# Inverse transforms in groups of four tiles, with one PSUM bank for each product

## The reference

```python
x = x + hyena(layernorm(x))          # out_w, out_b at its end
x = x + adapters(layernorm(x))       # 8 of 32 matrices W[ids], mixed by weights, and their bias

# hyena: v = short convolution of (x @ in_proj)[..., 0]; a filter h from a small network of the position
output = x_branches[i] * irfft(rfft(v, 2L) * rfft(h, 2L))[:, :L]    # only the last branch counts
return output @ out_w + out_b
```

## Time and profile before

| | |
|---|---|
| median of 3 runs | 2408.13 us (2402.51 to 2411.54) |
| the profiled execution | 2405.93 us, its span 2404.1 us |
| TensorE busy | 2314.3 us, 96% of the span |
| VectorE / ScalarE / GpSimd busy | 64% / 35% / 39% |
| the last stage | from about 1427 us to the end |

### The profile page before, as it was taken

The page is one execution under the profiler, slowest core; times in us unless marked ns, Lnnn a source line. Parts: engine busy times, 40 slices in busy tenths (PEclk is TensorE's granted clock), DMA queues, the critical chain, the costliest instruction groups (busy, mean ns, idle before and its releaser), DMA issues.

```text
span 2404.1 us, 39766 instructions
## 1 busy us (share of the span) xinstructions
PE 2314.3 (96%) x12804; PEld 1601.3 (67%) x12804; DVE 1547.2 (64%) x2187; ACT 843.4 (35%) x1151; POOL 946.2 (39%) x1190
## 2 busy tenths in 40 slices
PE   6679999999999999999999979999999999999998
PEld 2257777777777777644444426777777777777776
DVE  5834444443444344377777757888888888888886
ACT  3334444444444444344444432222222222222222
POOL 2322222222222222200000026777777777777774
PEclk9879999999999999999999989999999999999999
DMA  6634555445554555589999997855666665665663
GB/s 186 218 101 141 181 174 179 147 156 187 175 168 140 170 168 202 230 316 361 358 358 355 359 360 217 252 176 176 179 177 176 176 177 175 177 180 176 178 179 101
DMA packets 180517, 496.60 MB, mean 207 GB/s; under 512 B 19419, under 2 KB 19740, under 8 KB 159332
## 3 DMA queue, kind: packets, MB, share of 16 engines
q1 hardware_dynamic: 150756, 395.10, 51.3%
q10 hardware_dynamic: 29696, 100.68, 11.6%
HBM read 276.27 MB, written 219.43 MB: 206 GB/s over the span
## 4 chain that ended last, share of the span: by engine, by line
PE 52%; DVE 2%; issue 2%; DMA 1%; ACT 0%; DVEq 0%; POOL 0%; SPq 0%; POOLq 0%
PE m_psW L992 7%; PE m_psA L975 6%; PE b_psF L183 5%; PE b_psC L1290 5%; PE b_psF L184 5%; PE b_psO L184 5%; PE b_psO L183 5%; PE b_psO L185 5%; PE b_psF L185 5%; PE b_psP L1304 2%; PE b_psT L1321 2%; DVE m_m L1063 2%; DMA m_xin<-spec 1%; DMA spec<-wide_out 0%; DMA b_fin<-spec 0%
## 5 line engine op out<-in xcount | busy, mean ns | idle before, releaser
L1063 DVE TENSOR_TENSOR m_m<-m_psA,m_spec 128x1024 f32<-128x1024 f32 x256 | 295.4, 1215 | 110.5 <-PE m_psA L975 107.1
L720 POOL TENSOR_TENSOR vl<-v,vh 128x512 fp32r<-128x512 f32 x128 | 165.3, 1291 | 390.0 <-ACT vh L674 390.0
L1254 ACT ACTIVATE b_zh<-b_psT 128x512 fp32r<-128x512 f32 x128 | 76.4, 597 | 641.0 <-PE b_psT L1321 641.0
L992 PE MATMUL m_psW<-m_m,mats 64*64 64x512 f32 x2048 | 249.2, 589 | 0.0
L975 PE MATMUL m_psA<-m_xin,mats 64*64 64x512 f32 x1536 | 204.8, 598 | 11.2 <-DVE m_m L1063 5.5
L183 PE MATMUL psV<-wvh,nth 128*128 128x512 f32 x512 | 213.6, 417 | 0.6 <-DVE ntl L802 0.6
L821 DVE TENSOR_TENSOR gto<-psG,bgr 128x512 f32<-128x512 f32 x128 | 87.6, 685 | 195.4 <-PE psG L185 195.2
L183 PE MATMUL b_psO<-woh,b_oh 128*128 128x512 f32 x512 | 212.2, 414 | 0.0
L183 PE MATMUL b_psF<-wfh,b_zh 128*128 128x512 f32 x512 | 207.6, 406 | 2.8 <-DVE b_zl L1383 2.8
L184 PE MATMUL b_psO<-wol,b_oh 128*128 128x512 f32 x512 | 201.6, 394 | 0.0
L185 PE MATMUL b_psO<-woh,b_ol 128*128 128x512 f32 x512 | 201.4, 393 | 0.0
(11 more groups left out here) (126 smaller groups left out, 4696.4 us busy)
## 6 DMA issues: line engine op xcount, KB each, us to landing
spec<-wide_out SPq DMA_DIRECT2D x64, 1024.0 KB, 9.2
spec<-wide_out ACTq DMA_DIRECT2D x64, 1024.0 KB, 8.5
b_fin<-spec SPq DMA_DIRECT2D x128, 512.0 KB, 4.7
m_xin<-spec SPq DMA_DIRECT2D x30, 2048.0 KB, 11.9
xg<-in_L_attn_x_dram SPq DMA_DIRECT2D x64, 512.0 KB, 6.2
gate_d<-gto SPq DMA_DIRECT2D x32, 1024.0 KB, 3.9
b_gin<-gate_d SPq DMA_DIRECT2D x128, 256.0 KB, 3.6
b_xin<-in_L_attn_x_dram SPq DMA_DIRECT2D x256, 128.0 KB, 3.2
```

The source lines that it names most:

```text
L720: pool.tensor_tensor(vl[:, t % 2], v[:, t % 2], vh[:, t % 2].bitcast(F32), ALU.subtract).then_inc(v_lo, 1)
L992: mm = pe.matmul(psW[pair % 2][half[slot], q, :], ws[slot][half[q]], m[half[q], pair % RM, part, slot, :], start=part == 0, stop=part == 1)
L1063: dve.tensor_tensor(m[:, (k - 2) % RM, part], psA[k % RA][:], spec[:, par, part], ALU.mult).then_inc(m_done, 1)
```

## The change

The transforms of four tiles stand together in every fourth round (`conv_four`). Each of the four has a PSUM bank of its own; for these, psO and psF have one bank each instead of two. `b_fin` gets four buffers. All steps behind the transform have lags larger by three; `load_gate` and `load_x` have lag 2 instead of 0. `turn_w` uses the one bank of psO and the one of psF as scratch, so that the first project waits until that is over.

```diff
-            psC = [ps("b_psC0"), ps("b_psC1")]
+            psC = [ps(f"b_psC{i}") for i in range(4)]
-            psO = [ps("b_psO0"), ps("b_psO1")]
+            psO = ps("b_psO")
-            psF = [ps("b_psF0"), ps("b_psF1")]
+            psF = ps("b_psF")
+            psW = [psO, psF]
...
+            def fin_of(t):
+                return fin[:, t % 4] if t % 4 < 2 else fin_b[:, t % 4 - 2]
...
                 def load_conv(b, t):
...
-                    if old(b, t, 2):
-                        sp.wait_ge(c_ps, no(b, t) - 1)
+                    if old(b, t, 4):
+                        sp.wait_ge(c_ps, no(b, t) - 3)
...
-                pipelined(sp, B, T, [(load_conv, 0), (load_edges, 0), (load_gate, 0), (load_x, 0), (load_v0, 0)])
+                pipelined(sp, B, T, [(load_conv, 0), (load_edges, 0), (load_gate, 2), (load_x, 2), (load_v0, 0)])
...
-                pipelined(pool, B, T, [(correct, 0), (scalars, 3), (bias_y, 3)])
+                pipelined(pool, B, T, [(correct, 3), (scalars, 6), (bias_y, 6)])
...
-                pipelined(act, B, T, [(z_high, 4), (o_high, 1), (norm, 3), (w_high, 0), (store, 6)])
+                pipelined(act, B, T, [(z_high, 7), (o_high, 4), (norm, 6), (w_high, 0), (store, 9)])
...
                 def conv(b, t):
-                    pe.wait_ge(f_in[t % 2], 16 * (b * (T // 2) + t // 2 + 1))
-                    if old(b, t, 2):
-                        pe.wait_ge(a_done, no(b, t) - 1)
+                    pe.wait_ge(f_in[t % 4], 16 * (b * (T // 4) + t // 4 + 1))
+                    if old(b, t, 4):
+                        pe.wait_ge(a_done, no(b, t) - 3)
...
-                def conv_pair(b, t):
+                def conv_four(b, t):
...
-                    if t % 2:
-                        conv(b, t - 1)
-                        conv(b, t)
+                    if t % 4 == 3:
+                        for k in range(t - 3, t + 1):
+                            conv(b, k)
...
                 def project(b, t):
                     pe.wait_ge(o_lo, no(b, t) + 1)
-                    if old(b, t, 2):
-                        pe.wait_ge(y_done, no(b, t) - 1)
+                    if isinstance(b, int) and b * T + t == 0:
+                        pe.wait_ge(wf_lo, CT)
+                    if old(b, t, 1):
+                        pe.wait_ge(y_done, no(b, t))
...
                 def adapt(b, t):
...
-                    if old(b, t, 2):
-                        pe.wait_ge(res_done, no(b, t) - 1)
+                    if old(b, t, 1):
+                        pe.wait_ge(res_done, no(b, t))
...
-                pipelined(pe, B, T, [(conv_pair, 0), (turn_w, 0), (adapt, 5), (turn_z, 4), (turn_o, 1), (project, 2)])
+                pipelined(pe, B, T, [(conv_four, 0), (turn_w, 0), (adapt, 8), (turn_z, 7), (turn_o, 4), (project, 5)])
...
-                pipelined(dve, B, T, [(gate, 1), (residual, 3), (z_low, 4), (o_low, 1), (finish, 5), (bias_x, 0), (w_low, 0)])
+                pipelined(dve, B, T, [(gate, 4), (residual, 6), (z_low, 7), (o_low, 4), (finish, 8), (bias_x, 3), (w_low, 0)])
```

More of the change, by code:

```diff
@@ L1087, in back @@
             v0 = sb("b_v0", [P, B, C])
+            fin_b = sb("b_fin_b", [P, 2, 2, C])
             edge_b = sb("b_edge_b", [P, T - EARLY, 2, C])
@@ L1170, in load_conv @@
                         return
-                    if old(b, t, 2):
-                        sp.wait_ge(c_ps, no(b, t) - 1)
-                    sp.dma_start(fin[:, t % 2], spec3.rearrange("(r h t) b c -> b t r h c", h=2, t=T)[b, t]).then_inc(f_in[t % 2], 16)
+                    if old(b, t, 4):
+                        sp.wait_ge(c_ps, no(b, t) - 3)
+                    sp.dma_start(fin_of(t), spec3.rearrange("(r h t) b c -> b t r h c", h=2, t=T)[b, t]).then_inc(f_in[t % 4], 16)
                 def load_gate(b, t):
@@ L1263, in w_high @@
                         act.wait_ge(wf_ps, d + 1)
-                        act.activation(wfh[:, d], psF[d % 2][:], ACT.Copy).then_inc(wf_hi, 1)
-                pipelined(act, B, T, [(z_high, 4), (o_high, 1), (norm, 3), (w_high, 0), (store, 6)])
+                        act.activation(wfh[:, d], psW[d % 2][:], ACT.Copy).then_inc(wf_hi, 1)
+                pipelined(act, B, T, [(z_high, 7), (o_high, 4), (norm, 6), (w_high, 0), (store, 9)])
                 for i in range(D):
@@ L1281, in turn_w @@
                         for ot in range(CT):
-                            mm = pe.transpose(psF[d % 2][:, ot * P:(ot + 1) * P], res[:, ot, d * P:(d + 1) * P], ident[:])
+                            mm = pe.transpose(psW[d % 2][:, ot * P:(ot + 1) * P], res[:, ot, d * P:(d + 1) * P], ident[:])
                         mm.then_inc(wf_ps, 1)
                 def conv(b, t):
-                    pe.wait_ge(f_in[t % 2], 16 * (b * (T // 2) + t // 2 + 1))
-                    if old(b, t, 2):
-                        pe.wait_ge(a_done, no(b, t) - 1)
+                    pe.wait_ge(f_in[t % 4], 16 * (b * (T // 4) + t // 4 + 1))
+                    if old(b, t, 4):
+                        pe.wait_ge(a_done, no(b, t) - 3)
                     for h in range(2):
-                        mm = pe.matmul(psC[t % 2][h * N1:(h + 1) * N1, :], s4[:, h * T + t, :], fin[:, t % 2, h, :], start=True, stop=True)
+                        mm = pe.matmul(psC[t % 4][h * N1:(h + 1) * N1, :], s4[:, h * T + t, :], fin_of(t)[:, h, :], start=True, stop=True)
                     mm.then_inc(c_ps, 1)
-                def conv_pair(b, t):
-                    if t % 2:
-                        conv(b, t - 1)
-                        conv(b, t)
+                def conv_four(b, t):
+                    if t % 4 == 3:
+                        for k in range(t - 3, t + 1):
+                            conv(b, k)
                 def turn_o(b, t):
@@ L1308, in project @@
                     pe.wait_ge(o_lo, no(b, t) + 1)
-                    if old(b, t, 2):
-                        pe.wait_ge(y_done, no(b, t) - 1)
+                    if isinstance(b, int) and b * T + t == 0:
+                        pe.wait_ge(wf_lo, CT)
+                    if old(b, t, 1):
+                        pe.wait_ge(y_done, no(b, t))
                     for ct in range(CT):
-                        mm = mm3(pe, psO[t % 2][:], oh[:, t % 2, ct * P:(ct + 1) * P], ol[:, t % 2, ct * P:(ct + 1) * P],
+                        mm = mm3(pe, psO[:], oh[:, t % 2, ct * P:(ct + 1) * P], ol[:, t % 2, ct * P:(ct + 1) * P],
                                  woh[:, ct], wol[:, ct], ct == 0, ct == CT - 1)
@@ L1327, in adapt @@
                         pe.wait_ge(wf_lo, CT)
-                    if old(b, t, 2):
-                        pe.wait_ge(res_done, no(b, t) - 1)
+                    if old(b, t, 1):
+                        pe.wait_ge(res_done, no(b, t))
                     for ct in range(CT):
-                        mm = mm3(pe, psF[t % 2][:], zh[:, t % 2, ct * P:(ct + 1) * P], zl[:, t % 2, ct * P:(ct + 1) * P],
+                        mm = mm3(pe, psF[:], zh[:, t % 2, ct * P:(ct + 1) * P], zl[:, t % 2, ct * P:(ct + 1) * P],
                                  wfh[:, ct], wfl[:, ct], ct == 0, ct == CT - 1)
                     mm.then_inc(ff_ps, 1)
-                pipelined(pe, B, T, [(conv_pair, 0), (turn_w, 0), (adapt, 5), (turn_z, 4), (turn_o, 1), (project, 2)])
+                pipelined(pe, B, T, [(conv_four, 0), (turn_w, 0), (adapt, 8), (turn_z, 7), (turn_o, 4), (project, 5)])
             @block.vector
@@ L1343, in w_low @@
                         dve.wait_ge(wf_hi, d + 1)
-                        dve.tensor_tensor(wfl[:, d], psF[d % 2][:], wfh[:, d].bitcast(F32), ALU.subtract).then_inc(wf_lo, 1)
+                        dve.tensor_tensor(wfl[:, d], psW[d % 2][:], wfh[:, d].bitcast(F32), ALU.subtract).then_inc(wf_lo, 1)
                 def bias_x(b, t):
@@ L1353, in gate @@
                     dve.wait_ge(c_ps, no(b, t) + 1)
-                    dve.tensor_tensor(corr[:, t % 2], psC[t % 2][:], corr[:, t % 2], ALU.add).then_inc(a_done, 1)
+                    dve.tensor_tensor(corr[:, t % 2], psC[t % 4][:], corr[:, t % 2], ALU.add).then_inc(a_done, 1)
                     dve.wait_ge(a_done, no(b, t) + 1)
@@ L1370, in residual @@
                         dve.wait_ge(z_done, no(b, t) - 1)
-                    dve.tensor_tensor(y[:, t % 2], psO[t % 2][:], xin[:, t % D], ALU.add).then_inc(y_done, 1)
+                    dve.tensor_tensor(y[:, t % 2], psO[:], xin[:, t % D], ALU.add).then_inc(y_done, 1)
                     dve.wait_ge(y_done, no(b, t) + 1)
@@ L1389, in finish @@
                         dve.wait_ge(out_stored[t % D], 32 * (b * (T // D) + t // D))
-                    dve.tensor_tensor(res[:, t % D], psF[t % 2][:], yb[:, t % D], ALU.add).then_inc(res_done, 1)
-                pipelined(dve, B, T, [(gate, 1), (residual, 3), (z_low, 4), (o_low, 1), (finish, 5), (bias_x, 0), (w_low, 0)])
+                    dve.tensor_tensor(res[:, t % D], psF[:], yb[:, t % D], ALU.add).then_inc(res_done, 1)
```

(3 more changed lines are left out.)

## The result

The changed kernel takes 2413.73 us (median of 20 runs, 2405.13 to 2419.25), the kernel before 2407.60 us (median of 20 on the same chip). The ratio is 1.0024, 95% interval 1.0016 to 1.0031: 6 us slower, a quarter of a per cent. The forecast was 2418 us, with a range of 2396 to 2437. The interval excludes "no change", so the kernel is slower, but by less than the half per cent that the prediction used as its border: of its three cases "within 0.5%" came true, which had a chance of 0.40, where "slower" had 0.49.

What follows compares the result with a forecast made beforehand. TensorE's own order was taken as the bound (busy 868.00 of 868.00 us). 2405.9 - 13.1 + 25.4 - 4 + 1.5 = 2415.7, on the median's scale 2418 us; range 2396 to 2437.

Steps and rivals of the forecast that it cites:

- The group's price: TensorE, last stage: each group of transforms costs 0.41 us beyond its work; 32 fewer groups save 13.1 us.
- The rival of the slower adapt: TensorE's adapt after transforms: its extra 0.17 us follows the tiles, so only 7.7 us saved, 2423 us; chance 0.10.
- The late fourth load: SyncE's queue: each group's fourth-tile load, behind x loads waiting for y, comes 0.82 us late; 25 us over 31 groups.
- u: Time from the start of turn_z (TensorE's transpose of z) to the end of VectorE's y; taken as 0.5 us.
- VectorE's rest: VectorE around long rounds: a new long round of 10.2 us gives it 3 us of rest.
- The single banks: psO and psF: project waits for the previous tile's y, adapt for its res; slack thin, cost taken as nothing.
- The bound of 12 us: Upper bound for VectorE's chain slowing three short rounds in a row: 0.4 us per four rounds, 12 us in all.
- the border of u = 0.74: psO's bank: from u = 0.74 us on, project waits for y.
- The drift of 0.22 us a round: VectorE's chain from z_low to the next z_low takes 6.57 us, 0.22 us more than a short round.
- the second rival: psO and psF: the single banks bind as well, 0.4 us more in each four rounds, 2431 us; chance 0.20.
- The fill: Start of the last stage: first adapt about 3 us earlier with eight tiles done; -4 us, between -10 and +6.
- The drain: Last rounds: adapt waits for res of the tile before, 0.55 us in each; +1.5 us.

Runs made afterwards that it cites:

- experiment 1: The changed kernel with load_gate and load_x at lag 3 instead of 2: 2397.05 us, ratio 0.9950 to the kernel before.
- experiment 8: The changed kernel with load_gate and load_x at lag 1 instead of 2: 2657.51 us, ratio 1.1033 to the kernel before.
- experiment 2: The kernel before, pairs and old lags kept, with one PSUM bank instead of two for each of psO and psF: 2414.47 us, ratio 1.0023.
- experiment 4: The changed kernel with the first sequence's edge loads issued from ScalarE's queue instead of SyncE's: 2414.61 us, ratio 1.0029 to the kernel before.

## Why the prediction was right where it was, and where it was not

The forecast came within 5 us, by terms that were partly wrong against each other. Term by term:

- **The group's price**: right in place and size. 0.41 us was forecast, 0.38 to 0.42 measured; the excess goes with the group. 30 groups of four against 61 pairs behind the first adapt: 30 x 3.80 - 61 x 2.115 = -15.0 us, 1.7 of which are two tiles moved into the fill. So -13.3 us for 13.1 forecast. The rival of the slower adapt falls.
- **The late fourth load**: the mechanism was right, step by step (experiments 1 and 8); the size was 18.3 us where 25.4 stood, within its ends of 13 and 50. Three terms were off, and partly against each other. u was taken as 0.5 throughout; it was about -0.15 in 24 of 30 groups and 0.65 in 6, as in the loop the addition to xin in front of y is slowed less (0.81 us against 1.41). VectorE's rest alone doesn't decide it, for the groups outside the loop have the rest too. The issue behind y took 1.2 us in the last sequence and 1.44 to 1.59, once 2.3, in those of the loop, where 1.42 stood. And the load takes 4.5 to 5.5 us there, but up to 7.3 in the first sequence. The first sequence, with edge and v loads and a fall of the clock, was not costed at all, and its two groups have 10.1 of the 18.3 us; the next two, at u = 0.65 without such loads, have 2.2. The sum came out near by luck, with one part too dear and another missing. One figure beside it was miscounted: by its own terms (-13.1 - 4 + 1.5 against 31 x (u + 0.32)) gain and loss cancel at u = 0.18, not at 0.1.
- **The single banks**: costed at nothing; 1.7 us beyond 6.35 us were seen in the short rounds of the changed kernel (0.2 in five, 0.55 in one), 3.7 us in the long ones of experiment 2. The bound of 12 us was too wide, and the border of u = 0.74 too high: both products start 0.15 us behind the addition that frees their bank and not at once. The drift of 0.22 us a round, on which the second rival rested, doesn't add up: from round to round of a cycle u runs -3.8 (the rest in the long round), -0.5, -0.3, -0.15 in the loop, and -3.8, -0.7, 0.7, 0.65 outside it. In a round with y at 0.73 behind turn_z (1512.65) the project starts at 0.88 instead of 0.79, and then adapt starts 0.15 us behind the end of res, 3.74 us behind turn_z instead of 3.62, so that the round takes 6.58 us:

```profile
1515.56 0.68 DVE L1397 TENSOR_TENSOR b_res<-b_psF,b_yb 128x512 f32<-128x512 f32 x1
```

```profile
1516.39 0.47 PE L183 MATMUL b_psF<-wfh,b_zh 128*128 128x512 f32 x1
```

- **The fill**: -4 forecast, -2.0 seen: from the first transform to the first adapt 34.2 us instead of 34.5, with two tiles (1.7 us) more. These are single profiles, and experiments 1 and 4 had 32.1 and 31.5 us.
- **The drain**: 1.5 forecast, 4.2 seen. That adapt waits for res was right, as two waits longer by 0.7 us where three of 0.55 had been forecast; that they would let the clock fall at the very end was not thought of.
- **Sum**: -13.3 + 18.3 + 1.7 - 2.0 + 4.2 = +8.9 us. From the first transform to the last matmul the profiles have 969.0 and 977.6 us, +8.6. The medians differ by 6.1 us, as runs vary by several.

## What to carry to other kernels

When steps are moved by whole rounds, write down for each load in an in-order queue which wait stands in front of it and in which round of the other engine that wait ends. Here the tile arithmetic was right and free of waits on paper, and one round more of lag for two other loads was worth 17 us and turned a loss into a gain. A double buffer given up for a larger group is paid for where the pipeline runs empty, and in mid-stage wherever the freeing addition comes late: in both places the order on the engine that frees the bank decides, and moving one step forward got it back here (5 us). And the first pass of a loop, with its extra transfers, deserves a sum of its own.

## What the runs showed of the hardware

- VectorE's addition of two SBUF tensors of 128x512 in fp32 takes 0.68 us if it starts 0.04 us ahead of GpSimd's product. If it starts within an operation of GpSimd of that size, it takes the rest of that operation and 0.55 us more: so did all 189 that started at least 0.15 us before its end, in the last stage of the two profiles (0.81 us at 1906.15, 1.41 at 1481.62). GpSimd's operation that is already running keeps its 1.3 us; one of its two correction operations that starts while VectorE's addition or product of two SBUF tensors runs takes 1.5 to 1.8 us instead of 1.26 to 1.31. Who starts first is not slowed, so the cost depends on the phase between two engines: 60 us less of VectorE's busy time for the same work.
- The granted clock fell after an idle time of 3.3 us (to 0.59 in the next 3.5 us, 1.6 us lost) and after each of the two waits of 2.10 us at the end (0.64 in 2402 to 2406 us, 0.50 in 2410 to 2413). Waits of 0.69 and 1.28 us in mid-stage left it at 1.00, and so did the two of 1.41 us at the end of the kernel before.
